# Half of three groups of DMAs issued from ScalarE's queue, and a new instruction order, in a two-block convolution kernel

## What is computed

```
x = x + L0(_gn(x))
x = x + L1(_gn(x))
```

```
kern = jnp.exp(-(pu / sig_u) ** 2 - (ps / sig_s) ** 2)
w = mu * kern
w = w / (jnp.sum(w, axis=(1, 2), keepdims=True) + 1e-06)
agg = jnp.einsum('brsl,bcsl->brcl', w, patches).reshape(Bb, R * C, Hh, Ww)
return jnp.einsum('bkhw,ok->bohw', agg, pw_w) + pw_b[None, :, None, None]
```

## Time and profile before

| | |
|---|---|
| runs | 526.84, 529.3, 529.5 us; median 529.3 |
| profiled execution | 528.61 us, its span 526.8 us |
| TensorE busy | 469.2 us, 89% of the span |
| VectorE busy | 385.7 us, 73% |
| ScalarE busy | 188.9 us, 36% |
| GpSimd busy | 186.6 us, 35% |
| DMA | 32.22 MB, mean 61 GB/s |
| granted TensorE clock, mean | 0.973 |

### The profile page before, as it was taken

The page is one execution under the profiler, slowest core; times in us unless marked ns, Lnnn a source line. Parts: engine busy times, 40 slices in busy tenths (PEclk is TensorE's granted clock), DMA queues, the critical chain, the costliest instruction groups (busy, mean ns, idle before and its releaser), DMA issues.

```text
span 526.8 us, 7099 instructions
## 1 busy us (share of the span) xinstructions
PE 469.2 (89%) x2639; PEld 349.2 (66%) x2639; DVE 385.7 (73%) x530; ACT 188.9 (36%) x337; POOL 186.6 (35%) x93
## 2 busy tenths in 40 slices
PE   1348483899999999999999999999999999999995
PEld 1238363877846896588668884788568847884871
DVE  2599988989998988787698998799878973122101
ACT  3513322282236316541437142722464133330210
POOL 2152816704680553414640654074342710000000
PEclk9999885799999999999999999999999999999999
DMA  5100002601026111721261105410541026107301
GB/s 154 41 1 5 0 13 68 150 20 42 4 58 157 33 41 25 165 61 40 56 155 40 42 4 124 107 35 21 118 103 31 0 56 155 36 1 166 71 7 40
DMA packets 38225, 32.22 MB, mean 61 GB/s; under 512 B 24112, under 2 KB 28720, under 8 KB 38192
## 3 DMA queue, kind: packets, MB, share of 16 engines
q1 hardware_dynamic: 38192, 31.77, 25.5%
HBM read 5.66 MB, written 4.19 MB: 19 GB/s over the span
## 4 chain that ended last, share of the span: by engine, by line
PE 75%; DVE 13%; issue 6%; POOL 3%; ACT 2%; DMA 1%; SPq 0%; POOLq 0%; DVEq 0%
PE conv_ps L415 36%; PE conv_ps L423 16%; PE agg_ps L489 10%; DVE prod L1098 6%; PE val_ps L474 6%; PE geo_ps L456 3%; PE pw_ps L504 2%; POOL prod L1997 1%; POOL xs L2013 1%; PE conv_ps L437 1%; DVE ch L1018 1%; DVE prod L1108 1%; DVE ch L1016 1%; DMA xraw<-in_x 1%; DVE st L911 0%
## 5 line engine op out<-in xcount | busy, mean ns | idle before, releaser
L1098 DVE TENSOR_TENSOR prod<-val_ps,tapw 128x2048 f32<-128x2048 f32 x80 | 180.8, 2283 | 7.8 <-PE val_ps L474 7.1
L1997 POOL TENSOR_TENSOR prod<-prod 128x2048 f32<-128x2048 f32 x23 | 105.3, 4579 | 137.5 <-DVE prod L1098 137.5
L415 PE MATMUL conv_ps<-c_hi,wc_hi 128*128 128x448 f32 (+1 forms) x240 | 91.6, 382 | 0.0
L423 PE MATMUL conv_ps<-c,w_sb 128*64 128x512 f32 x384 | 90.3, 603 | 0.0
L2013 POOL TENSOR_TENSOR xs<-xn 128x1024 f32<-128x1024 f32 x32 | 69.8, 2192 | 48.5 <-DMA xn<-xn 21.3
L415 PE MATMUL conv_ps<-c_hi,wc_lo 128*128 128x448 f32 (+1 forms) x240 | 86.2, 359 | 0.0
L415 PE MATMUL conv_ps<-c_lo,wc_hi 128*128 128x448 f32 (+1 forms) x240 | 86.1, 359 | 0.0
L489 PEld LDWEIGHTS agg_ps<-ident_sb,prod 128*128 128x128 f32 x576 | 70.4, 150 | 23.3 <-issue 10.5
L489 PE MATMUL agg_ps<-ident_sb,prod 128*128 128x128 f32 x576 | 78.3, 288 | 8.1 <-DVE prod L1098 7.1
L415 PE MATMUL conv_ps<-xq,wc_hi 128*128 128x512 f32 x192 | 64.0, 414 | 0.1
L474 PE MATMUL val_ps<-ident_sb,xs 128*128 128x128 f32 x256 | 43.3, 296 | 18.8 <-DVE prod L1098 17.8
(11 more groups left out here) (109 smaller groups left out, 457.2 us busy)
## 6 DMA issues: line engine op xcount, KB each, us to landing
xq<-y SPq DMA_DIRECT2D x128, 132.0 KB, 2.6
xraw<-in_x SPq DMA_DIRECT2D x32, 128.0 KB, 2.8
x2r<-x SPq DMA_DIRECT2D x128, 32.0 KB, 1.9
out_y<-x2r SPq DMA_DIRECT2D x32, 128.0 KB, 2.8
w_sb<-in_w SPq DMA_DIRECT2D x1, 576.0 KB, 4.8
xn<-xn SPq DMA_DIRECT2D x16, 24.8 KB, 1.9
prod<-in_w SPq DMA_DIRECT2D x1, 384.0 KB, 3.3
prod<-in_w SPq DMA_DIRECT2D x1, 192.0 KB, 2.5
```

What stands on the lines that cost most here:

```text
L415: mm = nc.tensor.matmul(bank[:, 0:conv_cols(n)], weights, lo if part == 1 else hi, start=term == part == 0, stop=final and part == 2)
L423: mm = nc.tensor.matmul(bank[MID * rows:MID * rows + MID, :], w3_sb[:, at:at + MID], src, start=term == 0, stop=final)
L1098: v.tensor_tensor(dst, val.unsqueeze(2).to_broadcast([P, B, R, C]), wgt.unsqueeze(3).to_broadcast([P, B, R, C]), ALU.mult).then_inc(mult_d ...
L1997: p.tensor_tensor(product(i, TAPS * h + a), product(i, TAPS * h + a), product(i, TAPS * h + b), ALU.add).then_inc(add_g, 1)
```

## The change

Two things are changed. First, three groups of DMAs are shared out between SyncE and ScalarE, half each, the even ones on SyncE and the odd ones on ScalarE: the four loads of image 0, the sixteen slot transfers of image 0, and the four stores of image 7. All other images' DMAs stay on SyncE. ScalarE issues its two loads ahead of its first table load, its eight slot transfers (`first_slots`, behind a wait for the low part) between the first and the second `sums_out` of image 1, and its two stores at its end.

Second, the instruction lists of TensorE, VectorE, ScalarE and GpSimd are in another order; SyncE's list of calls is the same. The helpers that compute are not changed.

```diff
+        def queued(who, shared):
+            return range(4) if not shared else range(0, 4, 2) if who == "S" else range(1, 4, 2)
+
+        def send_slots(eng, who, i, g):
+            for s in queued(who, i == 0):
+                j0 = (2, 1, 1, 0)[s] + K8 * g
+                eng.dma_start(xq[C * s:C * s + C, :, j0:j0 + K8, :].bitcast(F32),
+                              y[C * g:C * g + C, :, (s + 1) % 2, :, :]).then_inc(xq_in[g], 16)
+
+        def send_rows(eng, who, j):
+            for s in queued(who, j == IMAGES - 1):
+                dst = out[j, :, :, :].rearrange("c (q s) w -> c q s w", s=4)[:, :, s, :]
+                eng.dma_start(dst, x2r[C * s:C * s + C, :, :]).then_inc(out_st, 16)
+
+        def send_image(eng, who, j):
+            for g in queued(who, j == 0):
+                eng.dma_start(xraw[C * g:C * g + C, j % 2, :],
+                              x[j, :, QR * g:QR * g + QR, :].rearrange("c r w -> c (r w)")).then_inc(x_in[j % 2], 16)
...
+                send_image(sp, "S", j)
...
+                send_slots(sp, "S", i, g)
...
+                send_rows(sp, "S", j)
...
+            def first_slots(i):
+                if i > 0:
+                    return
+                act.wait_ge(y_lo_done, 1)
+                for g in range(G):
+                    send_slots(act, "A", i, g)
+
+            def last_store(j):
+                if j < IMAGES - 1:
+                    return
+                act.wait_ge(out_done, 2 * j + 2)
+                send_rows(act, "A", j)
+
+            send_image(act, "A", 0)
...
             sums_out(1, 0)
+            first_slots(0)
...
+            last_store(7)
```

More of the change, by code:

```diff
@@ L539, in _ @@
             geometry(0)
+            gn1_sums(1, 0)
             values(0, 0)
-            gn1_sums(1, 0)
+            values(0, 1)
+            fold(0, 0)
             gn1_sums(1, 1)
-            fold(0, 0)
-            values(0, 1)
             values(0, 2)
@@ L575, in _ @@
             gn1_sums(2, 1)
-            values(1, 7)
             transpose_sums(1, 0)
             transpose_sums(1, 1)
+            values(1, 7)
+            geometry(2)
+            values(1, 8)
             transpose_sums(1, 2)
-            values(1, 8)
-            geometry(2)
+            values(1, 9)
+            convs(0, 0, 4)
             transpose_sums(1, 3)
[L583 to L586, removed]
             take_high(0, 0)
@@ L589, in _ @@
             pointwise(1, 0)
+            convs(0, 6, 7)
             take_high(0, 1)
-            convs(0, 6, 12)
+            values(2, 0)
+            convs(0, 7, 10)
             values(2, 1)
+            convs(0, 10, 12)
             transpose_sums(1, 4)
@@ L767, in _ @@
             gn1_sums(6, 1)
-            values(5, 6)
             convs(3, 36, 39)
             gn2_sums(4, 1)
-            convs(3, 39, 40)
+            convs(3, 39, 41)
             transpose_sums(5, 0)
-            convs(3, 40, 42)
+            convs(3, 41, 44)
             values(5, 7)
-            convs(3, 42, 45)
+            convs(3, 44, 45)
             values(5, 8)
+            geometry(6)
+            convs(3, 45, 48)
+            values(5, 9)
+            convs(3, 48, 49)
             transpose_sums(5, 1)
-            geometry(6)
@@ L835, in _ @@
-            take_high(5, 0)
+            convs(4, 25, 35)
+            values(6, 6)
+            convs(4, 35, 37)
+            gn2_sums(5, 1)
+            convs(4, 37, 40)
+            transpose_sums(6, 0)
+            values(6, 7)
+            gn1_sums(7, 0)
+            convs(4, 40, 42)
+            transpose_sums(6, 1)
+            values(6, 8)
+            convs(4, 42, 43)
+            gn1_sums(7, 1)
+            convs(4, 43, 47)
+            transpose_sums(6, 2)
+            geometry(7)
+            convs(4, 47, 51)
@@ L836, in _ @@
+            transpose_sums(6, 3)
+            convs(4, 51, 54)
+            convs(5, 0, 3)
+            values(6, 9)
+            convs(5, 3, 4)
+            take_high(5, 0)
+            convs(5, 4, 7)
+            transpose_sums(6, 4)
+            convs(5, 7, 8)
+            pointwise(6, 0)
+            transpose_sums(6, 5)
+            take_high(5, 1)
+            convs(5, 8, 9)
             values(7, 0)
-            convs(5, 4, 6)
-            transpose_sums(6, 4)
-            pointwise(6, 0)
@@ L854, in _ @@
-            convs(5, 22, 26)
-            values(7, 4)
-            convs(5, 26, 28)
+            convs(5, 13, 14)
+            take_high(5, 3)
+            convs(5, 14, 20)
+            values(7, 2)
+            convs(5, 20, 24)
+            values(7, 3)
+            convs(5, 24, 27)
+            values(7, 4)
+            convs(5, 27, 30)
+            transpose_sums(6, 7)
             values(7, 5)
-            convs(5, 28, 32)
+            convs(5, 30, 33)
             values(7, 6)
+            convs(5, 33, 36)
```

482 lines of the change are left out of this document (217 added, 265 removed).

## The result

Six runs of the changed kernel gave 531.79 to 533.09 us, median 532.84; the kernel before, on the same chip, a median of 529.15 in six runs, of which one, at 940.54 us, is left out of the ratio. The ratio is 1.0076, 95% interval 1.0055 to 1.0097: slower by 0.76%, some 4 us, where 3.45 us faster was forecast. The profiled execution took 533.09 us, its span 531.3 (before 528.61 and 526.8).

The account below looks back on a forecast made before the run. The prediction took waiting chains to bound the 103 us start-up and TensorE alone the convolution stream. Gains of 0.5 + 1.15 + 0.8 + 0.6 + 0.4 = 3.45 us from 528.61 gave 525.2 us, range 521.6 to 528.8.

Parts of the forecast that it names:

- rival of full engines: Split loads, slots and stores only fill the DMA engines' last tenth: 2.4 us gained, 526.2 us; chance 0.20.
- DMA share above 0.95: Sign that the forecast is right: DMA engines more than 0.95 busy during image 0's slot transfers.
- First image, 0.5 us gained: Image 0's loads, issued from two queues, let the statistics start earlier: 0.5 us, range 0.15 to 0.9.
- 58 to 77 us, 1.15 us gained: Start-up: values ahead of transposes let image 1's first product start when its tap weights are ready; range 0.8 to 1.2.
- 89 to 103 us, 0.8 us gained: Start-up: earlier transposes and split slot transfers start the first convolution at 100.4 to 101.6, not 102.81; range 0.2 to 1.4.
- eight issues of 0.6 us are covered: ScalarE's slot issues, 4.8 us, fit in the 8.7 us before its first high part; cover gone at 1.0 each.
- ScalarE blocked by its own issues: Rival: slow slot issues between 94.7 us and the first high part delay the convolution; 533.8 us at 2.08 each; chance 0.06.
- Tail, 0.6 us gained: Last four stores: two issues fewer in the row gain 0.6 us, range 0.4 to 1.3.
- Order from 103 us on, 0.4 us gained: Convolution stream: the new order removes 0.4 us of the 1.2 us TensorE wait on image 6's last product.
- bound of 2 us lost: Lower bound for the order from 103 us on; the upper was all 3.6 us of TensorE waits gained.
- given-back rival: Start-up's gain is lost in the middle to three new waits of 1 us: 528.2 us; chance 0.22.
- 0.36 + 0.12 + 0.10: Chance of a faster kernel, from the forecast, the full-engine case and the better case; given as about 0.59.

Follow-up runs that it names:

- e8: Kernel before, old order, with ScalarE issuing only four slot transfers of image 0, those the first convolution chunk needs; 529.98 us, ratio 1.0026.
- e6: Kernel before with the new order of the start-up up to 77 us only, all DMAs on SyncE; 527.21 us, ratio 0.9972.
- e4: Kernel before, old order, with only image 0's slot transfers split between SyncE and ScalarE; 531.93 us, ratio 1.0071.
- e2: Kernel before, old order, with loads, slot transfers and stores all split between SyncE and ScalarE; 531.70 us, ratio 1.0071.
- e5: Kernel before, old order, with only the last image's four stores split between SyncE and ScalarE; 529.21 us, ratio 1.0002.
- e1: Changed kernel with its new order but no split, every DMA on SyncE; 531.58 us, ratio 1.0054 to the kernel before.
- e10: e9 with one TensorE call moved: image 7's first norm sums ahead of a set of values and a group of transposes; 530.23 us, ratio 1.0029.
- e16: e6 with GpSimd's image 0 addition moved ahead of two pair sums, and the addition and pair sums held for VectorE's image 1 tap weights; 524.26 us, ratio 0.9909.
- e9: Kernel before with the new order only from image 2's geometry (about 101 us) on, all DMAs on SyncE; 531.99 us, ratio 1.0061.

## Why the prediction was wrong, and where it was right

Between the two profiled executions the five terms came out, in the order of the sum, at -0.5, +0.7, -1.3, 0 and -3.4 us: 4.5 us lost where 3.45 were to be gained. (The third runs from image 1's first product to the first convolution, the fifth from there to the last addition; the 1.04 us of transposes put off are counted in the third.) Three terms, loads, slots and stores, share one step that failed: a DMA share of 0.85 to 0.95 was read as room for more, with the 1.11 elsewhere as support. In none of the three did the transfers land sooner. The rival of full engines rests on the same reading, in its 0.15, 0.3 and 0.4. The sign "DMA share above 0.95" came true without the gain, and in e8 shares of 1.08 and 1.05 moved no more than one queue.

*First image, 0.5 us gained: wrong.* The issue did move forward by 0.9 us, and the landing did not follow. The full DMA engines, the lower bound of the term, were still too good.

*58 to 77 us, 1.15 us gained: right in mechanism, too large.* The product starts straight behind its tap weights, at 71.84, with the chain 0.5 us late from the load: 0.7 us gained, below the range of 0.8 to 1.2, since the tap weights came 0.4 us later, about the 0.3 that the term names and leaves out. In e6 the product is 0.83 us earlier.

*89 to 103 us, 0.8 us gained: the first failing step.* The transposes, geometry and values moved as worked out, but the slots did not. "By two queues the fourth on each begins at 96.6 and lands at 99.2", or 101.3 with full engines (its own numbers give 101.45), took an issue to cost 0.6 us whatever is under way, and a share of 1.0 to move transfers at one in 0.59 us. The issues cost 0.96 to 1.43 from the third or fourth in each queue on, the transfers stayed at one in 0.67 us, and the last slot that the first chunk needs landed at 102.78. Behind that wait of 2.96 us the clock fell to 0.50 once more, which the prediction had at nothing: 1.7 us, counted in the last term. For the same reason "eight issues of 0.6 us are covered" fell: at a median of 1.2 the cover of 1.0 was gone. The rival with a chance of 0.06, ScalarE blocked by its own issues, is what happens by itself in e4, but not at its place and price: there a median of 0.75 us an issue is enough, because TensorE waits for the copies of sums and not for the first high part. In the full change ScalarE's standing is hidden behind TensorE's own wait for the slots.

*Tail, 0.6 us gained: wrong.* Nothing, in the change (5.91 us), e2 (5.87) and e5 (6.18). A DMA share of 0.85 did not mean room for 0.15 more.

*Order from 103 us on, 0.4 us gained: the second failing step.* The rest is 4.4 us longer than before (422.52 against 418.11). Worked out from the rows: 1.04 is the group of transposes put off, which the prediction had counted; about 1.7 the half clock behind the wait for slots (three microseconds at 0.50, one at 0.79); 1.3 more idle time, since the two waits at 371 to 379 us, 2.3 together, came and the one of 1.2 in the earlier trace rows went, all of it and not the 0.4 that the term took. These make 4.0; the other 0.4 I cannot place. In e1, which waits 2.11 us for its slots and keeps the full clock, the rest is 3.15 longer than before, 2.1 without the transposes: just beyond the bound of 2 us lost. Of these losses e10 shows one cause, the norm sums: a VectorE instruction of 0.22 us that took 4.37. I looked only at which engine waits for which, took the durations of before as fixed, and so could not see that an order also decides which GpSimd instruction a VectorE instruction meets.

*The given-back rival* came true in kind, new waits where TensorE and VectorE are both near full, and was too small. (In the chances, 0.36 + 0.12 + 0.10 is 0.58 and not 0.59.)

## To carry to other kernels

Before a second engine shares out DMAs, look at the DMA share of that stretch: in this kernel, at 0.85 to 0.95, there was nothing to win, and ScalarE stood still while the transfers drained. Look also at which transfers are needed first: in e8 the queue that started later sent them behind others. When instructions are reordered, list for each GpSimd instruction the VectorE instructions that fall beside it, and look in the profile for short instructions with a maximum many times their median. A wait that holds GpSimd back, together with a new order of its own instructions, was worth some 3 us here (e16 against e6, 0.9909 and 0.9972 of before).

## What the runs showed of the hardware

- A VectorE instruction with two SBUF inputs that started while one of these GpSimd additions ran lasted until its end: 4.37 in place of 0.22 us, 2.47 in place of 0.28. The profile counts it as busy. One with a single input, L991, was held in the same way beside a pair sum: 1.20 us in place of 0.23. A VectorE product with one input in PSUM is not held: 2.27 us each beside the 4.53 us addition in e16. The Trainium skill, "SBUF — State Buffer", section "Who interferes with whom", states this of VectorE instructions with two SBUF inputs beside a GpSimd instruction that reads SBUF, an exclusive lock for the whole instruction; these traces agree.
- The sixteen slot issues of image 0, transfers of 132 KB, took 0.60 to 0.70 us in the one queue of the kernel before. In the two queues of the kernel after the first five took 0.60 to 0.74 and the others 0.96 to 1.43; in e4 ScalarE's took 0.62 to 1.03.
- The granted clock fell to 0.50 behind idle times of TensorE of 2.96 us (after) and 3.48 us (e4), and not behind 2.11 us (e1). In e9 it fell behind two waits of 1.2 and 1.1 us, and behind the same two in e1 and after it did not.
- The same program up to 101 us reached the first convolution at 101.90 (e9) and 103.62 us (e10): in e10 a VectorE instruction at 58.9 us was held out for 3.56 us, in e9 for 2.17.
